# A Fourier layer tower on one core: layer 0 from raw images held as rows, and batch statistics joined in one product

## The chip, the cores and the metric

The kernel runs on one core of a Trainium2 chip. The core has TensorE (PE, the matmul array, with its weight loads shown as PEld), VectorE (DVE), ScalarE (ACT), GpSimd (POOL) and SyncE (SP, which here issues the transfers). The metric is the device time of one execution in microseconds (us); lower is better.

## The reference

The input is 32 images of 64 x 64 pixels. A tower of four Fourier layers comes first, then a small transformer and a mixture of experts, which the change doesn't touch. The tower:

```python
h = concatenate([x, gx, gy])            # pixel, row position, column position
v = h @ p_w + p_b                       # 3 -> 32 channels: the lift
for i in range(4):
    x1 = irfft2(mix(rfft2(v)[12 + 12 low rows, 12 low columns], fw1[i], fw2[i]))
    x2 = einsum("bcxy,cd->bdxy", v, w_w[i]) + w_b[i]
    v = x1 + x2
    mean, var = over batch and pixels, for each channel
    v = (v - mean) * rsqrt(var + eps) * bn_g[i] + bn_b[i]
    if i < 3: v = relu(v)
out = v @ q_w + q_b
```

## The kernel before

All data are float32. `V` holds the activations: four quadrants of 32 partitions (a quadrant holds 16 of the 64 image rows x, a partition one channel), and along the row 16 chunks (one x each) of 32 images x 64 columns. Programs are written per engine, by hand, and semaphores order them; there is no scheduler.

A layer l runs in stages.

1. **Forward transforms** (layers 1 to 3): DVE transposes pairs of images of V (L541), PE transforms y (L760), DVE transposes (L548), PE transforms x (L772), DVE writes the spectra `MZ` (L555).
2. **Mixing**: for k = 0..5, 48 products of 64 x 64 by 32 columns (L864, two passes each, so 96 in the profile), after POOL has changed a sign in the mode weights of two ky (L403); DVE transposes the result (L583).
3. **Inverse**: PE transforms x (`inverse_x`, L885), DVE spreads it into `G` (L590), and 16 **units** (q, r) follow: PE adds the inverse in y (L900) and the channel product of V (L915) in PSUM, ACT moves the sum to V with the bias (L451, two halves), DVE takes the moments (L597, four per unit: 64 groups in all).
4. **Statistics**: `bn_aggr` over the 64 groups of a partition (L615), then the mean over the four quadrants by a product with `average` (L950), a difference and a square on DVE (L618 to L620), a second product for the mean of the squares (L952), variance (L622), square root on ACT (L456), reciprocal with one Newton step, gain and bias (L625 to L632). Only then can relu (ACT L430) start the next layer. This is done after layers 0, 1 and 2. Layer 3 has another way.

Layer 0 differs. Its input v is an affine map of three features, so its spectra come from the images' spectra: PE transforms the images (L739, L744), and for each of 12 ky DVE and POOL multiply the image's spectrum by the lift's row (L528, L412), DVE adds the fixed part of the position features (L531) and transposes (L533), and mixing of k waits for 2k + 2 of them (`s_min`). For the units' channel product V holds the four features (pixel, x, y, one) in rows 0..3 of each quadrant, as 16 transfers of 4 partitions (L360, 120 KB each), in part queued between the mode weights, and a last four (L373) that wait on SP for the spectra, since chunk 15 of V is workspace until then. PE waits for `s_feat[q]` and `s_feat_last` before a unit. The stationary operand is `lift_w`, 4 rows by 32.

## Time and profile before

| | us |
|---|---|
| median of 3 runs | 824.98 (822.92 to 828.79) |
| the profiled execution, its own time | 826.26 |
| its span, first to last instruction | 824.5 |
| PE busy | 631.6 (77%) |
| DVE busy | 576.0 (70%) |
| ACT busy | 362.3 (44%) |
| POOL busy | 72.1 (9%) |

Busy shares are means over stages with different limits, so the stages of layer 0 and the ends of layers are read from the timeline. In a timeline a row is the start, the length, the engine, the line, what is written from what, and in brackets how long the engine had been idle and what ended that. `f32 x96` in a PE row counts passes, two for a product of float32. A row of the view by windows gives busy time of each engine and the granted TensorE clock, as a share of 2.4 GHz.

### The profile page before, as it was taken

What the parts mean: (1) busy time and instruction counts of PE and PEld (TensorE: products, weight loads), DVE (VectorE), ACT (ScalarE), POOL (GpSimd) and SP (SyncE); (2) the same over time, 40 slices, a digit from 0 to 9 for tenths busy, and PEclk for the clock granted to TensorE, in tenths of its full rate; (3) what the DMA queues carried; (4) which work ended last, traced back from release to release, by engine and by line L of the source; (5) the groups of instructions that cost most, each with busy time, mean ns of one, the idle gap of its engine ahead of it and who ended that gap; (6) DMA issues with size and microseconds to landing.
All of it is one profiled execution on the core that took longest, in us unless ns stands there. A gap on an engine that the chain in (4) does not pass through costs nothing. (4 is left out here: it accounts for less than half of the span.)

```text
span 824.5 us, 25191 instructions
## 1 busy us (share of the span) xinstructions
PE 631.6 (77%) x11575; PEld 444.5 (54%) x11575; DVE 576.0 (70%) x896; ACT 362.3 (44%) x517; POOL 72.1 (9%) x112
## 2 busy tenths in 40 slices
PE   3447997466789992666799937788595899999997
PEld 2335775132477771333777723332434787787854
DVE  6852887699448776996468778988731868567453
ACT  0002545870014555900045545737222677767753
POOL 3601000000300000001100000002000222212200
PEclk9986998699879995999699978999987999999999
...
DMA packets 14809, 28.94 MB, mean 35 GB/s; under 512 B 5664, under 2 KB 6304, under 8 KB 14688
## 3 DMA queue, kind: packets, MB, share of 16 engines
...
q10 hardware_dynamic: 288, 0.73, 0.3%
...
## 5 line engine op out<-in xcount | busy, mean ns | idle before, releaser
L451 ACT ACTIVATE V<-ps,wts 128x1024 f32<-128x1024 f32 x96 | 101.8, 1111 | 285.7 <-PE ps L900 285.7
L597 DVE BATCH_NORM_STATS2 stats<-V 128x6 f32<-128x512 f32 x192 | 117.9, 676 | 31.9 <-ACT V L451 31.9
L900 PE MATMUL ps<-tab,A 64*128 64x128 f32 x1536 | 106.7, 285 | 28.8 <-DMA V<-in_grid 17.1
L900 PEld LDWEIGHTS ps<-tab,A 64*128 64x128 f32 x1536 | 93.6, 192 | 52.8 <-issue 37.4
L541 DVE STREAM_TRANSPOSE A<-V 128x2048 f32<-128x2048 f32 x48 | 107.2, 2270 | 6.2 <-ACT V L430 6.2
L430 ACT ACTIVATE V<-V,small 128x2048 f32<-128x2048 f32 x48 | 96.1, 2080 | 5.0 <-DVE small L632 5.0
L772 PE MATMUL ps<-A,tab 128*128 128x384 f32 x192 | 68.3, 499 | 33.2 <-DVE A L548 33.2
L760 PE MATMUL ps<-A,tab 32*32 32x512 f32 x1536 | 61.3, 655 | 38.6 <-DVE A L541 38.6
L590 DVE STREAM_TRANSPOSE A<-ps 128x2048 f32<-128x2048 f32 (+1 forms) x27 | 55.4, 2070 | 42.9 <-PE ps L885 42.9
L772 PEld LDWEIGHTS ps<-A,tab 128*128 128x128 f32 x192 | 34.4, 189 | 76.7 <-DVE A L548 62.0
L548 DVE STREAM_TRANSPOSE A<-ps 128x1024 f32<-128x1024 f32 x48 | 56.3, 1210 | 11.2 <-PE ps L760 11.2
L403 POOL TENSOR_SCALAR A<-A,tab 128x384 f32<-128x384 f32 x32 | 21.1, 662 | 474.2 <-DMA A<-in_modes 474.2
L760 PEld LDWEIGHTS ps<-A,tab 32*32 32x32 f32 x1536 | 21.4, 107 | 67.4 <-issue 65.5
L864 PE MATMUL ps<-MZ,A 64*64 64x32 f32 x1536 | 40.0, 270 | 17.2 <-issue 6.1
L864 PEld LDWEIGHTS ps<-MZ,A 64*64 64x64 f32 x1536 | 38.8, 197 | 19.5 <-issue 13.5
L915 PE MATMUL ps<-V,wts 32*32 32x256 f32 x2048 | 47.8, 385 | 0.0
L583 DVE STREAM_TRANSPOSE MZ<-ps 128x1024 f32<-128x1024 f32 x18 | 22.0, 1238 | 25.9 <-PE ps L864 25.9
L885 PE MATMUL ps<-tab,MZ 64*128 64x128 f32 x576 | 39.9, 291 | 0.0
L885 PEld LDWEIGHTS ps<-tab,MZ 64*128 64x128 f32 x576 | 37.6, 205 | 0.4 <-DVE MZ L583 0.2
L436 ACT ACTIVATE ps<-ps,small 128x1024 f32<-128x1024 f32 x20 | 21.7, 1087 | 30.5 <-PE ps L782 30.5
L915 PEld LDWEIGHTS ps<-V,wts 32*32 32x32 f32 x2048 | 25.9, 103 | 10.4
L1286 POOL TENSOR_SCALAR hT<-h0T,wl 128x256 f32<-128x256 f32 x32 | 17.6, 564 | 153.4 <-DVE h0T L1433 153.4
...
## 6 DMA issues: line engine op xcount, KB each, us to landing
...
A<-in_turned SPq DMA_DIRECT2D x1, 512.0 KB, 3.6
...
```

The lines of the kernel that those rows point to most:

```text
L430: nc.scalar.activation(pair, pair, ACT.Relu, bias=bias, scale=scale).then_inc(s_relu, 1)
L451: nc.scalar.activation(Vm[:, 2 * h:2 * h + 2, r, 512 * q:512 * (q + 1)], bank(half_of_u(q, r) + 2 * h, 2).rearrange("p (m n) -> p m n", m= ...
L541: nc.vector.transpose(T[n % 3].rearrange("p (k n) -> p k n", k=16), Vk[:, :, P * n:P * (n + 1)]).then_inc(s_T, 1)
L548: nc.vector.transpose(Y[:, 1024 * p:1024 * (p + 1)].rearrange("p (c i k) -> p c i k", i=4, k=8), src).then_inc(s_Y, 1)
L590: nc.vector.transpose(G[quad % 4].rearrange("p (i x o) -> p i x o", i=4, o=CH)[:, :, 4 * r0:4 * r1], bank(half_of_x(quad), 4).rearrange("p ...
L597: last = nc.vector.bn_stats(stats[:, 16 * q + 4 * r + m, :], Vm[:, m, r, 512 * q:512 * (q + 1)])
L760: last = nc.tensor.matmul(bank(i)[Q * j:Q * (j + 1), :].rearrange("p (s k c) -> p s k c", s=2, k=8), fwd_y[rows, Q * yh:Q * (yh + 1)], T3[ ...
L772: last = nc.tensor.matmul(bank((4 if l == L - 1 else 4 + 2 * (u % 2)) + pair)[:, 0:MODES * CH], fwd_x[layout][ri], y[:, :, MODES * ri:MODE ...
L864: last = nc.tensor.matmul(out.rearrange("p (i b) -> p i b", b=2), W[ky][rows, kx, :], src, start=True, stop=True, tile_position=(64 * kxh, ...
L885: last = nc.tensor.matmul(ps[:, at:at + P], MZ[rows, 1024 * k + P * quad:1024 * k + P * (quad + 1)], inv_x[layout][rows, :], start=True, s ...
L900: last = nc.tensor.matmul(ps[:, at:at + P], G[(2 * q + quad) % 4][rows, x:x + P], inv_y[rows, :], start=step < 2 and quad == 0, stop=step ...
L915: nc.tensor.matmul(out, kernel[rows, :], src, start=False, stop=False, tile_position=(Q * i, Q * j))
```

## The change

**Layer 0's features.** The four features are no longer loaded into V. Chunk 15 of V takes `l_pixels`: in each quadrant 16 rows of images (one row for each x), two rows of ones and a row of y, one transfer of 1 MB over 128 partitions. The stationary operand of a unit's channel product is one of 16 slices of `lift_k` (19 rows by 32 columns), which POOL makes from the lifted weights and a table of ones and zeros that picks the unit's x. `lift_k` lies where the weights of ky 3 were, so SP holds the load of layer 1's ky 3 until the last unit of layer 0.

**Layer 0's spectra.** PE transforms the images in x with their spectra as stationary operand, so that the pairs of images come out along partitions, and adds the positions' part in the same bank by three products of 12 rows. A product of 19 rows by 32 columns by 512 (the pairs' rows and three fixed rows, against `lift_rows`) then gives the lifted spectrum in PSUM, 48 of them for the 12 ky, and DVE transposes six blocks of 1,024 from PSUM into MZ. POOL has no part in it, and mixing of k waits for min(k + 3, 6) of the blocks.

**Transfers.** The table of spectra goes ahead of the weights, `lift_rows` (256 KB) has a semaphore of its own, and the 12 loads of mode weights go without a break, then the mask and the pixels.

**Statistics** (layers 0 to 2). The first 48 groups are aggregated while the last row of units runs, and written back as one triple (count, mean, count x variance). After the last unit DVE aggregates this triple and the 16 groups left, spreads (1, mean, variance) over four column groups by quadrant, one product with `average` brings all quadrants' triples to every partition, and a second `bn_aggr` over 12 values in PSUM joins them. The square root on ACT reads that directly. Products are fused, so that five operations follow it in place of eight. The last unit's moments start after the first half of ACT's move.

The rows that the prediction speaks of, first PE at the start of layer 0, before:

```order
L736 MATMUL ps<-wts,stats 128x32
L739 MATMUL ps<-A,tab 32x512 x4
L744 MATMUL ps<-V,tab 128x192 x2
L864 MATMUL ps<-MZ,r_ky 64x32 x96
L864 MATMUL ps<-MZ,A 64x32 x192
L885 MATMUL ps<-tab,MZ 128x128 x24
```

and now:

```order
L746 MATMUL ps<-A,tab 32x512 x4
L749 MATMUL ps<-wts,stats 128x32
L752 MATMUL ps<-V 128x128 x3
L758 MATMUL ps<-tab,V 128x128 x6
L772 MATMUL ps<-V 32x512 x48
L892 MATMUL ps<-MZ,r_ky 64x32 x96
L892 MATMUL ps<-MZ,A 64x32 x192
```

57 products stand where 2 stood ahead of the mixing, and the lift went behind the images' transform. On DVE, from the last moments of layer 0 on, before:

```order
L597 BN_STATS stats<-V 128x6 x24
L615 BN_AGGR small<-stats 128x2
L618 COPY small<-ps 128x2
L619 TENSOR_TENSOR small<-small 128x1
L620 TENSOR_TENSOR small<-small 128x1
L622 TENSOR_SCALAR small<-ps,small 128x1
L625 RECIPROCAL small<-small 128x1
L626 TENSOR_TENSOR small<-small 128x1
```

(L627 to L632 follow, six more) and now:

```order
L592 BN_STATS stats<-V 128x6 x12
L598 BN_AGGR small<-stats 128x2
L599 MEMSET stats 128x1
L600 COPY stats<-small 128x1
L601 TENSOR_SCALAR stats<-small 128x1
L592 BN_STATS stats<-V 128x6 x12
L621 BN_AGGR small<-stats 128x2
L623 SCALAR_TENSOR_TENSOR small<-small,tab 128x12
L628 BN_AGGR small<-ps 128x2
L630 TENSOR_SCALAR small<-small 128x1
L631 TENSOR_SCALAR small<-small 128x1
L633 RECIPROCAL small<-small 128x1
```

(L634 to L639 follow, four more). Four operations moved ahead of the last 12 moments.

The diff, cut:

```diff
+    pixels = np.zeros((4, Q, BATCH, S), np.float32)
+    pixels[:, 0:16] = image[:, where, :].transpose(1, 2, 0, 3)
+    pixels[:, 16:18] = 1.0
+    pixels[:, 18] = np.linspace(0.0, 1.0, S, dtype=np.float32)
+    pixels = pixels.reshape(P, BATCH * S)
...
+    lift_rows = np.zeros((4, Q, PAIRS, CH), np.float32)
+    for i in range(PAIRS):
+        lift_rows[:, i, i] = p_w[0]
+    for f, row in enumerate((p_w[1], p_w[2], p_b)):
+        lift_rows[:, 16 + f] = row
+    lift_rows = lift_rows.reshape(P, PAIRS * CH)
...
+        room = V[:, BLK * 13:BLK * 15]
+        l_yt, l_spec, l_rows, l_grid, l_mask = (room[:, a:b] for a, b in ((0, 1024), (1024, 1408), (1408, 1920), (1920, 2432), (2432, 2448)))
+        l_pixels = V[:, BLK * 15:BLK * 16]
+        lift_k = r_ky[:, KW * 3:KW * 3 + 16 * CH]
...
             sp.dma_start(l_turned, turned).then_inc(s_const, 16)
             sp.dma_start(tab[:, :], table[:, 0:T_ALL]).then_inc(s_const, 16)
+            sp.dma_start(l_grid[0:12, :], grid_spectra).then_inc(s_const, 16)
             sp.dma_start(lift, weights[:, 0:P]).then_inc(s_const, 16)
             sp.dma_start(wts[:, :], weights[:, P:P + W_PARAMS + N_PARAMS]).then_inc(s_const, 16)
-            sp.dma_start(l_rows, lift_rows).then_inc(s_const, 16)
-            sp.dma_start(l_grid, grid_spectra).then_inc(s_const, 16)
+            sp.dma_start(l_rows, lift_rows).then_inc(s_rows, 16)
...
-            for ky in range(RING):
+            for ky in range(MODES):
                 load_modes(0, ky)
-            load_features(0)
-            for ky in range(RING, MODES):
-                load_modes(0, ky)
...
-            sp.wait_ge(s_min, MODES)
...
+            sp.dma_start(l_mask, grid).then_inc(s_mask, 16)
+            sp.dma_start(l_pixels, pixels).then_inc(s_feat, 16)
             for l in range(1, L):
                 for ky in range(RING):
                     sp.wait_ge(s_mix, KYP * (l - 1) + ky // 2 + 1)
+                    if l == 1 and ky == RING - 1:
+                        sp.wait_ge(s_U, 2 * UNITS)
                     load_modes(l, ky)
...
+            nc.gpsimd.memset(l_yt, 0.0).then_inc(s_pad, 1)
+            pool.wait_ge(s_const, 80)
+            for ky in range(MODES):
                 negate(0, ky)
-            pool.wait_ge(s_lspec, 1)
-            for ky in range(MODES):
...
-                if ky >= RING:
-                    negate(0, ky)
+            pool.wait_ge(s_lyt, 2)
+            pool.wait_ge(s_mask, 16)
+            pool.wait_ge(s_mix, 2)
+            nc.gpsimd.tensor_tensor(lift_k.rearrange("p (k c) -> p k c", c=CH), lift_w[:, :].unsqueeze(1).broadcast_to([P, 16, CH]),
+                                    l_mask.unsqueeze(2).broadcast_to([P, 16, CH]), ALU.mult).then_inc(s_lift_k, 1)
...
-                act.wait_ge(s_bn, 3 * l + 3)
-                nc.scalar.activation(small[:, 10:11], small[:, 9:10], ACT.Sqrt).then_inc(s_sqrt, 1)
+                act.wait_ge(s_bn, 2 * l + 2)
+                nc.scalar.activation(small[:, 10:11], small[:, 3:4], ACT.Sqrt, bias=small[:, 23:24]).then_inc(s_sqrt, 1)
...
             nc.vector.tensor_scalar(small[:, 17:18], bn_bias[L - 2], 0.0, None, ALU.max).then_inc(s_shift, 1)
-            fixed, term = (t.rearrange("p (k c) -> p k c", c=CH) for t in (l_fixed, l_term))
+            nc.vector.memset(small[:, 20:21], 1.0)
+            link(nc.vector.memset(small[:, 23:24], EPS))
+            dve.wait_ge(s_lift, 1)
+            dve.wait_ge(s_pad, 1)
+            nc.vector.transpose(l_yt.rearrange("p (k i) -> p i k", i=Q)[:, 0:PAIRS, :],
+                                bank(0).rearrange("p (i x) -> p i x", x=Q)).then_inc(s_lyt, 1)
             dve.wait_ge(s_lift, 2)
-            nc.vector.transpose(l_yt.rearrange("p (k i) -> p i k", i=PAIRS),
-                                bank(0).rearrange("p (i x) -> p i x", x=Q)).then_inc(s_lyt, 1)
             nc.vector.tensor_copy(lift_w[:, :], bank(2)[:, 0:CH]).then_inc(s_lyt, 1)
...
-            dve.wait_ge(s_lspec, 1)
-            for ky in range(MODES):
-                grid3 = l_grid3[ky % 2].rearrange("p (i c) -> p i c", c=CH)
-                if ky % 3:
-                    dve.wait_ge(s_lift0, ky - ky // 3)
-                else:
...
-                link(nc.vector.tensor_tensor(grid3, grid3, l_fixed[:, CH * ky:CH * (ky + 1)].unsqueeze(1).broadcast_to(three),
-                                             ALU.add))
-                nc.vector.transpose(MZ[:, 512 * ky:512 * (ky + 1)], l_grid3[ky % 2]).then_inc(s_min, 1)
+            for k in range(KYP):
+                dve.wait_ge(s_outer, k // 2 + 1)
+                nc.vector.transpose(MZ[:, 1024 * k:1024 * (k + 1)], bank((4 + 2 * k) % 8, 2)).then_inc(s_min, 1)
...
                 def moments(q, r):
-                    dve.wait_ge(s_V, 2 * (UNITS * l + 4 * q + r + 1))
                     for m in range(4):
+                        if m == 0 or q == OCT - 1 and r == 3 and m == 2:
+                            dve.wait_ge(s_V, 2 * (UNITS * l + 4 * q + r) + (1 + m // 2 if q == OCT - 1 and r == 3 else 2))
                         last = nc.vector.bn_stats(stats[:, 16 * q + 4 * r + m, :], Vm[:, m, r, 512 * q:512 * (q + 1)])
                     last.then_inc(s_stats, 1)
+                def moments_so_far():
+                    dve.wait_ge(s_stats, UNITS * l + UNITS - 4)
+                    link(nc.vector.bn_aggr(small[:, 2:4], groups[:, 0:6 * 48]))
+                    nc.vector.memset(so_far[:, 0:1], 48.0 * 512.0)
+                    nc.vector.tensor_copy(so_far[:, 1:2], small[:, 2:3])
+                    nc.vector.tensor_scalar(so_far[:, 2:3], small[:, 3:4], 48.0 * 512.0, None, ALU.mult).then_inc(s_sofar, 1)
...
-                nc.vector.bn_aggr(small[:, 2:4], stats[:, :, :].rearrange("p n s -> p (n s)")).then_inc(s_bn, 1)
-                dve.wait_ge(s_bn, 3 * l + 1)
-                dve.wait_ge(s_avg, 2 * l + 1)
-                link(nc.vector.tensor_copy(small[:, 5:7], bank(0)[:, 0:2]))
-                link(nc.vector.tensor_tensor(small[:, 7:8], small[:, 2:3], small[:, 5:6], ALU.subtract))
-                nc.vector.tensor_tensor(small[:, 4:5], small[:, 7:8], small[:, 7:8], ALU.mult).then_inc(s_bn, 1)
-                dve.wait_ge(s_avg, 2 * l + 2)
-                nc.vector.tensor_scalar(small[:, 9:10], bank(1)[:, 0:1], small[:, 6:7], EPS, ALU.add, ALU.add).then_inc(s_bn, 1)
-                dve.wait_ge(s_bn, 3 * l + 3)
+                dve.wait_ge(s_sofar, l + 1)
+                link(nc.vector.bn_aggr(small[:, 21:23], groups[:, 6 * 48 - 3:]))
+                nc.vector.scalar_tensor_tensor(out=small[:, 24:36].rearrange("p (q n) -> p q n", n=3),
+                                               in0=small[:, 20:23].unsqueeze(1).broadcast_to([P, 4, 3]), scalar=4.0,
+                                               in1=pick[:, 0:Q:8].unsqueeze(2).broadcast_to([P, 4, 3]),
+                                               op0=ALU.mult, op1=ALU.mult).then_inc(s_bn, 1)
+                dve.wait_ge(s_avg, l + 1)
+                nc.vector.bn_aggr(small[:, 2:4], bank(0)[:, 0:12]).then_inc(s_bn, 1)
+                dve.wait_ge(s_bn, 2 * l + 2)
+                nc.vector.tensor_scalar(small[:, 9:10], small[:, 3:4], EPS, None, ALU.add)
+                link(nc.vector.tensor_scalar(small[:, 5:6], small[:, 2:3], -1.0, None, ALU.mult))
                 dve.wait_ge(s_sqrt, l + 1)
                 link(nc.vector.reciprocal(small[:, 11:12], small[:, 10:11]))
...
-                nc.vector.tensor_tensor(small[:, 1:2], bn_bias[l], small[:, 12:13], ALU.subtract).then_inc(s_norm, 1)
+                link(nc.vector.scalar_tensor_tensor(out=small[:, 12:13], in0=small[:, 11:12], scalar=small[:, 11:12], in1=small[:, 9:10],
+                                                    op0=ALU.mult, op1=ALU.mult))
+                link(nc.vector.tensor_scalar(small[:, 13:14], small[:, 12:13], -0.5, 1.5, ALU.mult, ALU.add))
+                link(nc.vector.scalar_tensor_tensor(out=small[:, 0:1], in0=small[:, 13:14], scalar=small[:, 11:12], in1=bn_gain[l],
+                                                    op0=ALU.mult, op1=ALU.mult))
+                nc.vector.scalar_tensor_tensor(out=small[:, 1:2], in0=small[:, 0:1], scalar=small[:, 5:6], in1=bn_bias[l],
+                                               op0=ALU.mult, op1=ALU.add).then_inc(s_norm, 1)
...
-            nc.tensor.matmul(bank(2)[:, 0:CH], lift, conv_w[0], start=True, stop=True).then_inc(s_lift, 1)
+            pe.wait_ge(s_const, 80)
             for j in range(4):
                 b2, xh = j // 2, j % 2
                 last = nc.tensor.matmul(bank(0)[Q * j:Q * (j + 1), :], front_y[:, Q * b2:Q * (b2 + 1)],
                                         l_turned[:, 512 * xh:512 * (xh + 1)], start=True, stop=True)
             last.then_inc(s_lift, 1)
+            nc.tensor.matmul(bank(2)[:, 0:CH], lift, conv_w[0], start=True, stop=True).then_inc(s_lift, 1)
+            for g in range(3):
+                nc.tensor.matmul(bank(1)[:, P * g:P * (g + 1)], l_grid[0:12, 0:P], l_grid[0:12, P * (g + 1):P * (g + 2)],
+                                 start=g == 0, stop=False)
             pe.wait_ge(s_lyt, 1)
-            for ri in range(2):
-                last = nc.tensor.matmul(bank(1)[:, 0:MODES * PAIRS], fwd_x[0][ri],
-                                        l_yt[:, MODES * PAIRS * ri:MODES * PAIRS * (ri + 1)], start=ri == 0, stop=ri == 1)
+            for g in range(3):
+                for ri in range(2):
+                    at = Q * (MODES * ri + 4 * g)
+                    last = nc.tensor.matmul(bank(1)[:, P * g:P * (g + 1)], l_yt[:, at:at + P], fwd_x[0][ri],
+                                            start=False, stop=g == 2 and ri == 1)
             last.then_inc(s_lift, 1)
+            pe.wait_ge(s_lspec, 1)
+            pe.wait_ge(s_rows, 16)
+            for g in range(3):
+                if g == 1:
+                    pe.wait_ge(s_lyt, 2)
+                if g == 2:
+                    pe.wait_ge(s_min, 2)
+                for j in range(4):
+                    for k in range(4):
+                        rows = slice(Q * k, Q * k + SPEC_ROWS)
+                        last = nc.tensor.matmul(bank((4 + 4 * g) % 8 + k)[Q * j:Q * (j + 1), :],
+                                                l_spec[rows, P * g + Q * j:P * g + Q * (j + 1)], l_rows[rows, :],
+                                                start=True, stop=True, tile_position=(Q * k, Q * j))
+                last.then_inc(s_outer, 1)
...
                     if l == 0:
-                        pe.wait_ge(s_min, 2 * k + 2)
+                        pe.wait_ge(s_min, min(k + 3, KYP))
...
-                                rows = slice(Q * i, Q * i + depth)
+                                rows = slice(Q * i, Q * i + (Q if l else PIXEL_ROWS))
                                 out = bank(base + i)[Q * j:Q * (j + 1), :].rearrange("p (s h n) -> p h s n", s=2, h=2)[:, half]
-                                src = Vm[rows, j, r, 512 * q:512 * (q + 1)].rearrange("p (s h n) -> p h s n", s=2, h=2)[:, half]
-                                nc.tensor.matmul(out, kernel[rows, :], src, start=False, stop=False,
+                                src = (Vm[rows, j, r] if l else l_pixels[rows, :])[:, 512 * q:512 * (q + 1)]
+                                chunk = 4 * j + r
+                                kernel = conv_w[l][rows, :] if l else lift_k[rows, CH * chunk:CH * (chunk + 1)]
+                                nc.tensor.matmul(out, kernel, src.rearrange("p (s h n) -> p h s n", s=2, h=2)[:, half],
+                                                 start=False, stop=False,
                                                  tile_position=(Q * i, Q * j))
...
-                    if l == 0:
-                        pe.wait_ge(s_feat[q], 64)
-                        pe.wait_ge(s_feat_last, 64)
+                    if l == 0 and q == 0:
+                        pe.wait_ge(s_feat, 16)
+                        pe.wait_ge(s_lift_k, 1)
...
-                pe.wait_ge(s_bn, 3 * l + 1)
-                nc.tensor.matmul(bank(0)[:, 0:2], average, small[:, 2:4], start=True, stop=True).then_inc(s_avg, 1)
-                pe.wait_ge(s_bn, 3 * l + 2)
-                nc.tensor.matmul(bank(1)[:, 0:1], average, small[:, 4:5], start=True, stop=True).then_inc(s_avg, 1)
+                pe.wait_ge(s_bn, 2 * l + 1)
+                nc.tensor.matmul(bank(0)[:, 0:12], average, small[:, 24:36], start=True, stop=True).then_inc(s_avg, 1)
...
```

## Rows read from the trace of the kernel before

**Rows 1.** Timeline (start us, length us, engine, line, operation): DVE at the start of layer 0

```profile
15.98 0.71 DVE L533 STREAM_TRANSPOSE MZ<-A 128x512 f32<-128x512 f32 x1
...
39.75 0.71 DVE L533 STREAM_TRANSPOSE MZ<-A 128x512 f32<-128x512 f32 x1
```

**Rows 2.** Timeline, layer 0 up to its first unit

```profile
7.72 1.94 PE L739 MATMUL ps<-A,tab 128*32 128x512 f32 x8
...
7.98 0.58 POOL L403 TENSOR_SCALAR r_ky<-r_ky,tab 128x384 f32<-128x384 f32 x1 [7.54 <-DMA r_ky<-in_modes]
...
10.82 1.65 PE L744 MATMUL ps<-V,tab 128*128 128x192 f32 x4 [1.16 <-DVE lift_w L515]
...
12.50 0.32 ACT L425 COPY V<-ps 128x192 f32<-128x192 f32 x1 [10.48 <-PE ps L744]
...
22.47 2.78 PE L864 MATMUL ps<-MZ,r_ky 64*64 64x32 f32 x96 [1.58 <-DVE MZ L533]
...
41.74 5.27 PE L864 MATMUL ps<-MZ,A 64*64 64x32 f32 x192 [5.95 <-DVE MZ L583]
...
48.92 4.58 DVE L590 STREAM_TRANSPOSE A<-ps 128x2048 f32<-128x2048 f32 x3 [0.59 <-PE ps L885]
...
67.27 2.08 PE L900 MATMUL ps<-tab,A 64*128 64x128 f32 x16 [17.06 <-DMA V<-in_grid]
```

**Rows 3.** Timeline, the same products in other stretches

```profile
155.31 4.08 PE L760 MATMUL ps<-A,tab 32*32 32x512 f32 x64 [8.99 <-DVE A L541]
...
159.43 2.38 DVE L548 STREAM_TRANSPOSE A<-ps 128x1024 f32<-128x1024 f32 x2 [2.07 <-PE ps L760]
...
164.15 2.34 PE L760 MATMUL ps<-A,tab 32*32 32x512 f32 x64 [0.57 <-DVE A L541]
...
397.32 2.90 PE L864 MATMUL ps<-MZ,A 64*64 64x32 f32 x101 [0.68 <-issue]
...
581.37 1.59 PE L864 MATMUL ps<-MZ,A 64*64 64x32 f32 x96
```

**Rows 4.** Busy time by windows (start:end, length, engines, PEclk, DMA share, GB/s)

```profile
18.00:34.00 16.00, 9.35 (x327) 8.98 (x328) 11.98 (x17) 0.00 (x0) 9.41 (x10) 1.00 0.57 154
...
67.00:77.00 10.00, 9.73 (x130) 8.26 (x132) 0.73 (x1) 2.12 (x2) 2.35 (x4) 0.50 0.05 18
216.00:220.00 4.00, 2.06 (x125) 1.95 (x126) 2.02 (x2) 0.00 (x0) 1.54 (x3) 1.00 1.01 384
396.00:400.00 4.00, 3.32 (x126) 3.20 (x124) 1.31 (x2) 0.00 (x0) 1.63 (x4) 0.50 0.54 177
580.00:584.00 4.00, 3.12 (x127) 2.47 (x126) 2.91 (x9) 0.90 (x2) 0.00 (x0) 1.00 0.01 4
```

**Rows 5.** Timeline, first unit of layer 1 and last moments of layers 1 and 0

```profile
241.90 1.16 PE L900 MATMUL ps<-tab,A 64*128 64x128 f32 x16 [2.21 <-DVE A L590]
...
310.73 2.47 DVE L597 BATCH_NORM_STATS2 stats<-V 128x6 f32<-128x512 f32 x4 [0.94 <-ACT V L451]
...
140.00 2.47 DVE L597 BATCH_NORM_STATS2 stats<-V 128x6 f32<-128x512 f32 x4 [0.94 <-ACT V L451]
```

**Rows 6.** Timeline, the statistics after layer 0

```profile
137.84 2.12 ACT L451 ACTIVATE V<-ps,wts 128x1024 f32<-128x1024 f32 x2 [1.29 <-PE ps L900]
...
142.50 1.89 DVE L615 BATCH_NORM_AGGREGATE small<-stats 128x2 f32<-128x384 f32 x1
...
145.14 0.16 DVE L618 COPY small<-ps 128x2 f32<-128x2 f32 x1 [0.75 <-PE ps L950]
...
146.92 0.16 DVE L625 RECIPROCAL small<-small 128x1 f32<-128x1 f32 x1 [0.34 <-ACT small L456]
...
148.47 31.88 ACT L430 ACTIVATE V<-V,small 128x2048 f32<-128x2048 f32 x16 [1.65 <-DVE small L632]
```

**Rows 7.** Groups by line (busy us, mean ns of one): two small operations of DVE

```profile
L648 DVE BATCH_NORM_AGGREGATE small<-A 128x2 f32<-128x144 f32 x1 | 0.8, 805 | 0.0
...
L689 DVE SCALAR_TENSOR_TENSOR small<-small 128x1 f32<-128x1 f32 x1 | 0.2, 219 | 0.0
```

107 lines of the change are left out of this document (38 added, 69 removed).

## The prediction, made before the result was known

> **What bounds the kernel now.** I read the timeline of layer 0 first, then the windows for TensorE's clock, then the end of each layer 0 to 2, because the change touches nothing else. In layer 0 DVE makes the twelve lifted spectra in a row, the first transpose at 15.98 and the last at 39.75 [rows 1]; mixing follows block by block and ends at 41.74 + 5.27 = 47.01 [rows 2]. DVE's first two spreads of the inverse would let the units begin at about 48.92 + 4.58 x 3/4 = 52.4. They begin at 67.27, and the row says why: 17.06 us idle, ended by the last feature transfer [rows 2]. So two things set the start of the units, a DVE chain and, on top, the 4-partition transfers. From the first unit to the last moments layer 0 takes 140.00 - 67.27 = 72.7 us, layer 1 takes 310.73 - 241.90 = 68.8 us [rows 2, 5] for the same units. The 3.9 us between them are the clock: it is 0.50 from 67 to 77 [rows 4], after the wait, and L900's first 16 passes take 2.08 us where they take 1.16 at the full clock [rows 2, 5].
>
> After the last unit nothing overlaps. ACT ends at 137.84 + 2.12 = 139.96, relu starts at 148.47 [rows 6]: 8.5 us, three times in the kernel, all on the path.
>
> **The clock in layer 0 needs care.** The window 18 to 34 shows 1.00, but 96 mixing passes take 2.78 us there, 29 ns each [rows 2, 4]. At 397, in a window at 0.50, they take 2.90/101 = 29 ns, and at 581, in one at 1.00, 1.59/96 = 17 ns [rows 3, 4]. So I take these early passes as run at 1.2 GHz, and the 1.00 as a value that stands before the first recorded change. The Trainium skill, "TensorE: Matmul & The Clock Gate", section "What's actually happening", says that the throttled state is the default and that activity releases it; by that rule the array starts slow, and the durations agree while the printed clock does not. Were the 1.00 right, the mixing would stay at 2.78 us per block, which is a rival below.
>
> **The change, layer 0.** Its new path, step by step.
>
> - Constants. The images' transform starts at 7.72, behind the lift's product; now it is first and the last constants are issued one transfer earlier. I take 6.9, and 1.94 us at the same price [rows 2]: 8.8. The first transpose and the gap before L744 cost 10.82 - 9.66 = 1.2 us; the lift and the three products of the positions fit in that gap. 10.0.
> - Spectra in x: 12 passes of 128 columns where there were 4 of 192 in 1.65 us [rows 2], 0.41 each. By columns that is 0.27, by passes 0.41: 3.3 to 4.9 us, and I take 3.6, since mixing passes with short streams go far faster. 13.6. ACT's copy takes 0.32 for 192 columns and now has 384, 0.5: 14.1.
> - Lifted spectra: 96 passes of 32x32 tiles by 512. 64 such passes take 4.08 us slow and 2.34 at full clock [rows 3], so a third (32) is 2.04 or 1.17. Rows used (19 or 32) don't appear in a pass's length: units with 4 rows and with 32 both give the steady pace of the moments. Two thirds end at 18.2. DVE transposes 1,024 from PSUM in 2.38/2 = 1.19 [rows 3]; the first two blocks are out at 18.6, the third part is then written by 20 to 21, and mixing can begin, as it needs only three blocks. This replaces the 24 us of rows 1. The last three transposes lie beside it.
> - Mixing: six blocks without a wait for DVE. In the trace the clock rose somewhere in the 5.27 us of back-to-back mixing, and at the latest with the 4.08 us of L760 [rows 2, 3]. Early rise: 20 + 6 x 1.59 = 29.5. Late rise: 21.2 + 5.3 for two blocks, then 4 x 1.59 = 32.9. I take 31.
> - Mode weights: twelve loads of 384 KB at the 384 GB/s of the window at 216 [rows 4] take 12.3 us behind the 256 KB of rows, so the last lands near 20.5; POOL needs 0.58 for each sign change [rows 2]. Mixing at one block per 1.59 us is never ahead of them. Mask and pixels (1 MB, 2.8 us) land by 24. `lift_k` is one POOL operation of 512 columns after the twelve sign changes, done before 28. Both are hidden by the mixing; without that cover they would move the first unit one for one.
> - Units: from the end of mixing 52.4 - 47.0 = 5.4 us, so the first at 36.4, and with a warm array layer 1's 68.8 us: last moments at 105.2 instead of 140.0. **Gain 34.8 us** (33 to 36.5 by the two clock cases).
> - SP holds the load of layer 1's ky 3 until the units are done. It is used at about 180, and only loads that wait for the forward stage stand behind it. POOL's sign changes after it wait too, but nothing asks for them earlier. Zero.
>
> **The change, statistics.** In the last row of units each group of moments follows 0.94 us of idle DVE [rows 5]. The early aggregation has 288 values. Two sizes give 1.89 us for 384 and 0.805 for 144 [rows 6, 7], thus 0.156 + 4.5 ns per value: 1.45 us, and with three small operations about 2.0. It eats the first idle stretch and 1.1 us more; the second is eaten by that, so the last moments begin when the half of ACT's last move is there, near 139.2, and end at 141.6 in place of 142.5. Aggregation of 99 values: 0.60, ends 142.2. The spread product 0.2. PE and its way back take 145.14 - 144.39 = 0.75 [rows 6]: 143.2. Aggregation of 12 values 0.21: 143.4. The root on ACT lies beside two scalar operations: reciprocal at 143.8 (before: 146.92). Eight operations took 148.47 - 146.92 = 1.55; five remain, three of them with a pointer scalar at 0.219 [rows 7], 1.15 us. Relu at 144.9: **3.5 us less**, 10.6 for three layers. Bounds: 2.5 (aggregation from PSUM or of few values dearer than the line through the two sizes) and 4.2 each.
>
> **Sum.** 826.26 (the profiled execution's own time) - 34.8 - 10.6 = 780.9. The median before is 1.3 lower, which I leave inside the range. **781 us.**
>
> **Rivals.**
> 1. The array gains no speed in the mixing of layer 0, either as the printed 1.00 is true there or as the clock does not rise. For it: the window of rows 4. Against: 29 ns against 17 ns. Six blocks take 16.7: mixing ends at 37.9, units at 43.3 to 44.1, gain 27 to 28. Total 788.
> 2. A transfer takes the place of the one removed. If the twelve loads do not reach 384 GB/s but half of it, weights and pixels land near 38, mixing ends at 34.5, units start near 40. Gain 31. Total 785.
> 3. The statistics give little: the early aggregation delays the last moments, or `bn_aggr` from PSUM is dear. 1.5 us each: total 787.
> 4. Slower than before: the units' channel products, with one image block read by four column tiles and 19 rows of weights that change with every tile, leave the array at 1.2 GHz for all of layer 0's units. L900 shows the price, 2.08/1.16 = 1.79; on 68.8 us that is +54 us, total 835. It decides against the change once 45.4/54 = 84% of the stage runs slow. For it: the first unit ran slow for 10 us though PE was busy 9.73 of them [rows 4]. Against: it did speed up with 4 rows, and 32 rows in layer 1 keep the clock.
>
> **Chances.** Forecast (774 to 787) 0.76, rivals 0.10, 0.05, 0.06, 0.03. The range 773 to 794 leaves out rival 4, a fast end where everything is at its bound, and two rivals together. A measurement here can't tell less than about 1% (8 us) from no change: faster 0.97, same 0.01, slower 0.02.
>
> **What would show it.** The first L926 row (the units' first) near 36 with a DVE releaser, not a DMA; no row of DVE between the lift's copy and the six transposes from PSUM; mixing of 96 passes at about 1.6 us in most blocks; 16 units in 68.8 us; ACT's last move to relu in 5.0 us instead of 8.5. The forecast is wrong if the first unit waits for pixels or `lift_k`, if mixing waits for mode weights, or if the clock falls between outer products and units.

## The result, and the profile after

| | before | changed |
|---|---|---|
| median of 4 runs, us | 826.47 (822.92 to 828.79) | 788.89 (787.36 to 796.71) |
| ratio | | 0.957, 95% interval 0.953 to 0.961 |
| profiled execution, us (span) | 826.26 (824.5) | 787.36 (785.6) |
| first unit of layer 0 begins | 67.27 | 43.74 |
| ACT's last move of layer 0 ends | 139.96 | 112.52 |
| relu of layer 0, 1, 2 begins | 148.47, 319.20, 489.59 | 117.35, 284.14, 452.62 |

The kernel is 4.3% faster; 781 us was forecast. Of the span's 38.9 us, 27.4 lie ahead of the last move of layer 0, 3.7 between that and relu, 3.9 and 1.9 in layers 1 and 2, and 1.9 in all that follows. The stretch from move to relu is 3.7 shorter in layers 1 and 2 as well (279.31 to 284.14 and 447.79 to 452.62, 4.83 us each); layer 2 gave only 1.9 since its way from layer 1's relu to its own last move took 163.65 us, where it was 161.88.

The start of layer 0 now, from the timeline (start us, duration us, engine, line, operation, tiles, count, and in brackets the idle time ahead with what ended it). It answers to [rows 1, 2].

```profile
7.01 1.93 PE L746 MATMUL ps<-A,tab 128*32 128x512 f32 x8 [7.01 <-DMA wts<-in_weights]
11.02 2.93 PE L758 MATMUL ps<-tab,V 128*128 128x128 f32 x12
13.98 0.48 ACT L435 COPY V<-ps 128x384 f32<-128x384 f32 x1 [11.97 <-PE ps L758]
14.51 4.09 PE L772 MATMUL ps<-V 19*32 19x512 f32 x64 [0.57 <-ACT V L435]
16.71 7.01 DVE L526 STREAM_TRANSPOSE MZ<-ps 128x1024 f32<-128x1024 f32 x6 [6.57 <-PE ps L772]
19.15 2.02 PE L772 MATMUL ps<-V 19*32 19x512 f32 x32 [0.55 <-DVE MZ L526]
21.10 5.35 PE L892 MATMUL ps<-MZ,r_ky 64*64 64x32 f32 x192
26.24 8.17 PE L892 MATMUL ps<-MZ,A 64*64 64x32 f32 x288
35.02 2.79 PE L892 MATMUL ps<-MZ,A 64*64 64x32 f32 x96 [0.61 <-issue]
37.73 3.71 PE L913 MATMUL ps<-tab,MZ 64*128 64x128 f32 x48
40.15 4.58 DVE L583 STREAM_TRANSPOSE A<-ps 128x2048 f32<-128x2048 f32 x3 [1.04 <-PE ps L913]
43.74 1.16 PE L926 MATMUL ps<-tab,A 64*128 64x128 f32 x16 [2.31 <-DVE A L583]
44.84 1.49 PE L943 MATMUL ps<-V,r_ky 19*32 19x256 f32 x64
```

DVE's 24 us chain and the wait for the last feature transfer are gone: the first unit is released by DVE's spread of the inverse, and its 1.16 us for 16 passes says full clock. The mixing begins at 21.10, the late end of the forecast's 20 to 21.2. It does not end where it was forecast: 576 passes from 21.10 to 37.81, 29 ns each on average, with one pause of 0.61 us, and no group of them faster than 27.9 ns.

The end of layer 0, same view, answers to [rows 6].

```profile
104.72 1.44 DVE L598 BATCH_NORM_AGGREGATE small<-stats 128x2 f32<-128x288 f32 x1
109.14 4.88 DVE L592 BATCH_NORM_STATS2 stats<-V 128x6 f32<-128x512 f32 x8 [0.36 <-ACT V L461]
110.40 2.12 ACT L461 ACTIVATE V<-ps,wts 128x1024 f32<-128x1024 f32 x2 [1.29 <-PE ps L926]
114.05 0.60 DVE L621 BATCH_NORM_AGGREGATE small<-stats 128x2 f32<-128x99 f32 x1
114.92 0.60 PE L979 MATMUL ps<-small,tab 128*128 128x12 f32 x2 [4.11 <-DVE small L623]
115.56 0.21 DVE L628 BATCH_NORM_AGGREGATE small<-ps 128x2 f32<-128x12 f32 x1 [0.69 <-PE ps L979]
116.20 0.16 DVE L633 RECIPROCAL small<-small 128x1 f32<-128x1 f32 x1 [0.18 <-ACT small L466]
117.35 4.08 ACT L440 ACTIVATE V<-V,small 128x2048 f32<-128x2048 f32 x2 [1.25 <-DVE small L639]
```

From the end of ACT's last move (112.52) to relu: 4.83 us where it was 8.51. Each aggregation lies on the line through the two sizes of before: 1.44, 0.60 and 0.21 us for 288, 99 and 12 values, from PSUM as from SBUF.

### The profile page after: what moved, and what is told of

Same layout as the page of the kernel before. It is cut to its first block and busy times, and to the rows that moved or that the text cites. A ratio compares the mean times of both kernels' runs of the same rounds, so it can differ in the third digit from the quotient of the medians.

```text
span 785.6 us, 25353 instructions
## 1 busy us (share of the span) xinstructions
PE 637.4 (81%) x11679; PEld 445.4 (57%) x11679; DVE 558.0 (71%) x874; ACT 362.5 (46%) x517; POOL 60.5 (8%) x106
## 5 line engine op out<-in xcount | busy, mean ns | idle before, releaser
L926 PE MATMUL ps<-tab,A 64*128 64x128 f32 x1536 | 104.3, 281 | 13.6 <-ACT V L461 7.8
L926 PEld LDWEIGHTS ps<-tab,A 64*128 64x128 f32 x1536 | 91.1, 187 | 37.4 <-issue 22.2
L801 PE MATMUL ps<-A,tab 128*128 128x384 f32 x192 | 70.0, 509 | 33.0 <-DVE A L541 33.0
L416 POOL TENSOR_SCALAR A<-A,tab 128x384 f32<-128x384 f32 x32 | 18.7, 586 | 393.1 <-DMA A<-in_modes 393.1
L892 PEld LDWEIGHTS ps<-MZ,A 64*64 64x64 f32 x1536 | 39.2, 199 | 10.8 <-issue 9.9
L943 PEld LDWEIGHTS ps<-V,wts 32*32 32x32 f32 x2048 | 25.9, 103 | 10.4
## 6 DMA issues: line engine op xcount, KB each, us to landing
V<-in_pixels SPq DMA_DIRECT2D x1, 1024.0 KB, 12.6
```

What stands on the lines that cost most here:

```text
L801: last = nc.tensor.matmul(bank((4 if l == L - 1 else 4 + 2 * (u % 2)) + pair)[:, 0:MODES * CH], fwd_x[layout][ri], y[:, :, MODES * ri:MODE ...
L892: last = nc.tensor.matmul(out.rearrange("p (i b) -> p i b", b=2), W[ky][rows, kx, :], src, start=True, stop=True, tile_position=(64 * kxh, ...
L926: last = nc.tensor.matmul(ps[:, at:at + P], G[(2 * q + quad) % 4][rows, x:x + P], inv_y[rows, :], start=step < 2 and quad == 0, stop=step ...
L943: nc.tensor.matmul(out, kernel, src.rearrange("p (s h n) -> p h s n", s=2, h=2)[:, half], start=False, stop=False, tile_position=(Q * i, Q ...
```

## Experiments: the parts alone

All are compared with the kernel before on the same chip. The first four undo or keep one part.

**The statistics alone**, on the kernel before.

```diff
+ # before with: moments_so_far(), the spread by quadrant, one product with average,
+ # the second bn_aggr, the fused products; layer 0 as it was
```

> The kernel before with the statistics of the change alone. Theory (the two halves of the change are worth what their stretches show): ACT's last move to relu takes 4.8 us instead of 8.5 after layers 0, 1 and 2, the start of layer 0 is as before (first unit at about 67), so 11 us less than before, near 815. Rival (the shorter idle of TensorE after the units changes its clock in the next forward stage): more than 13 or less than 8 us.

817.62 us (815.53 to 818.77), ratio 0.989 (0.986 to 0.992). Relu of layer 0 at 146.61, which is 1.9 us earlier in this execution, where the units' first wait and their slow clock are still there (66.57 and 2.08 us for 16 passes); the units took 2.5 us longer in this execution (the granted clock fell again at 95.9 and its mean from 96 to 112 is 0.79), so the last move ends at 141.79, 1.8 later than before, and from there to relu it is 4.82 us. The part is worth 3.7 us from move to relu in each of the three layers, 11 in all as expected, and 10.8 by the medians of these runs (828.38 before). The spans of the two profiled executions differ by 9.1 only, because of those units.

**Both parts of layer 0, old statistics**, and each of the two alone.

```diff
  # lift_only:    the change without its statistics
  # rows_only:    before + l_pixels and lift_k (spectra still by POOL and DVE)
  # spectra_only: before + lifted spectra by TensorE (features still 4 rows a quadrant)
```

> The changed kernel with the old statistics, so layer 0's rows and spectra alone. Theory: first unit near 44 as in the changed kernel, relu of layer 1 at about 121, 27.5 us less than before, near 799; with the statistics' 11 us that adds up to the change's 38.9. Rival (the two halves help each other through the clock): the two alone add up to less than 35 or more than 43.

> The kernel before with the features held as rows (one load of 1 MB, lift_k by POOL) and nothing else; the spectra are lifted by DVE and POOL as before. Theory (a transfer and a DVE chain stand one behind the other): the wait of 17 us for features goes, the first unit starts when the spreads are out, 48 to 52.4, and the slow first 10 us of the units go too if the array has just worked: 15 to 23 us less than before, near 806. Rival (the transfers were only the last of several waits): first unit after 58, less than 10 us.

> The kernel before with the spectra lifted by TensorE and nothing else; features are loaded into V by 16 transfers of 4 partitions as before. Theory: mixing is over by 40 or so, but the first unit still waits for features, which land near 60 to 67, and the array has gone slow by then: 0 to 7 us less than before, near 822. Rival (the features were late only since the last four waited for the spectra): first unit near 45, 20 us or more less.

| | median us | ratio (95%) | first unit |
|---|---|---|---|
| both | 802.53 | 0.972 (0.968 to 0.975) | 45.65 |
| rows alone | 806.93 | 0.976 (0.973 to 0.979) | 48.78 |
| spectra alone | 829.07 | 1.000 (0.997 to 1.003) | 66.15 |

The first units of these three, from their timelines:

```profile
45.65 1.16 PE L909 MATMUL ps<-tab,A 64*128 64x128 f32 x16 [2.30 <-DVE A L581]
```

```profile
48.78 1.66 PE L904 MATMUL ps<-tab,A 64*128 64x128 f32 x16 [2.30 <-DVE A L595]
```

```profile
66.15 2.08 PE L914 MATMUL ps<-tab,A 64*128 64x128 f32 x16 [25.56 <-DMA V<-in_grid]
```

The bracket decides each. The rows alone came as expected (near 806, first unit from 48 to 52.4), the spectra alone at the low end of 0 to 7 us. The spectra alone finish their mixing at 37.4 and then wait 25.56 us for the features, so they gain nothing; the rows alone remove that wait, and DVE's chain shows up behind it at 48.8. Nearly all of the gain is the rows' as long as both are counted from before, and the spectra's share, 3 to 5 us, exists only once the rows are in: two limits in parallel, of which the later one hides the other. The times of both parts and of the rows alone overlap in their intervals; the 3.1 us between their first units carry this. (Constants landed 1.5 us later in the run with both parts, 8.49 instead of 7.01, which is most of why its unit begins at 45.65 and not at 43.74.)

Do the two halves add up? Both parts of layer 0 were expected at 799 us and took 802.5. By medians they gave 25.9 us and the statistics 10.8, 36.6 together, where the change has 37.6. By the spans of the profiled executions it is 22.6 and 9.1, 31.7 of 38.9, which is below the 35 that the rival named. The rows tell where this goes: 1.5 us to the late constants, 2.5 to the slow units of the run above, and 4.2 to layers 1 and 2 of this one, whose ways from relu to last move took 163.5 and 164.8 us instead of 162.2 and 161.9. None of it lies in a stretch that a half changes, so nothing here shows the halves helping each other.

**No early aggregation**: all 384 values after the last unit.

```diff
-                    if q == OCT - 1:
-                        moments_so_far()
-                link(nc.vector.bn_aggr(small[:, 21:23], groups[:, 6 * 48 - 3:]))
+                link(nc.vector.bn_aggr(small[:, 21:23], groups))
```

> The changed kernel with all 64 groups aggregated after the last unit, the early aggregation left out, the rest of the new statistics kept. Theory (by aggregation at 0.156 us + 4.5 ns per value): 1.89 in place of 0.60, +1.3 us per layer, +3.9 in all; the early one costs nothing since the last moments wait for ACT. Rival (the early aggregation delays the last moments by part of its 2.0 us): less than +0.8 per layer.

Three runs of 791.41 to 798.37 us, ratio 0.961 (0.953 to 0.969); a fourth took 3138.08 us and is left out. The times can't tell it from the change. The rows can: last move ends at 112.70, aggregation of 384 values 1.89 us, relu at 118.82, thus 6.12 us against 4.83. The early part is worth 1.3 us in layer 0, as expected.

## Experiments: why the mixing stayed at 29 ns a pass

The forecast had the mixing speed up to 17 ns. Two theories: the clock never rose for it, or something else holds it. One run above already has the rise. With the spectra alone the clock came up inside the mixing, and yet it took from 21.02 to 37.39, 16.4 us; its last block:

```profile
35.79 1.60 PE L879 MATMUL ps<-MZ,A 64*64 64x32 f32 x96 [0.59 <-issue]
```

Ahead of this block, too, TensorE had stood, 1.01 us with no wait named and 0.55 us for POOL.

**Repeat the second third of the outer products** three times, to give the array more to do ahead of the mixing.

```diff
-                for j in range(4):
+                for j in list(range(4)) * (3 if g == 1 else 1):
```

> The changed kernel with the second third of the outer products done three times over (the same values into the same bank), which adds 4.1 us of dense work ahead of the mixing, of which 0.5 lie in a wait. Theory 1 (the clock): dense products raise it before the mixing, whose passes then take 17 ns instead of 29; +3.0 and -6.7 and -0.7, first unit near 39, total 4 us less than the changed kernel. Rival (not the clock): +3.5 us.

793.37 us, ratio 0.958 (0.953 to 0.962). 160 outer passes took 9.87 us, 62 ns each, then the mixing 24.40 to 40.86 at 29 ns; the first unit at 47.36 was slow too. The 4 us less of theory 1 did not come; the time is 4.5 us above the changed kernel, nearer to the rival's 3.5 more. In this execution the clock had not come up by then, so the run says nothing on a mixing at full clock.

**Products of zeros while the constants load.** DVE's clearing of the banks leaves out banks 4 to 7 here.

```diff
+            pe.wait_ge(s_pad, 1)
+            for n in range(40):   # 32 x 32 x 512, operands zero, into banks 4 to 7
+                nc.tensor.matmul(bank(4 + i)[Q * j:Q * (j + 1), :], l_yt[rows, 0:Q], l_yt[rows, 512:1024], ...)
```

> The changed kernel with 40 products of zeros (32x32 tiles by 512 columns, into banks that the start no longer clears by DVE) on TensorE while the constants load, 1.7 to about 6.9 us. Theory 1 (layer 0's mixing takes 29 ns a pass since the array is at its lower clock and mixing alone does not raise it): the array is at full clock by the first product or soon after and stays there, mixing passes take 17 ns, the first unit starts near 34 instead of 43.7, total 9 us less than the changed kernel. Theory 2 (the sparse stretch between 9 and 14.5 us lets it fall again): no gain. Rival (mixing in layer 0 is held by fresh weights or by the transfers, not by the clock): the first products are faster, mixing keeps 29 ns.

788.16 us, ratio 0.953 (0.949 to 0.957). From its timeline (the first row is the images' transform, 1.93 us in the changed kernel), and its windows (PE, PEld, DVE, ACT, POOL busy us and count, granted clock, DMA share, GB/s):

```profile
8.06 1.07 PE L752 MATMUL ps<-A,tab 128*32 128x512 f32 x8 [1.20 <-DMA wts<-in_weights]
12.53 2.35 PE L778 MATMUL ps<-V 19*32 19x512 f32 x64 [0.57 <-ACT V L435]
16.29 2.02 PE L778 MATMUL ps<-V 19*32 19x512 f32 x32 [1.42 <-DVE MZ L526]
18.25 4.15 PE L898 MATMUL ps<-MZ,r_ky 64*64 64x32 f32 x145
```

```profile
14.50:16.00 1.50, 0.37 (x15) 0.00 (x0) 1.50 (x2) 0.00 (x0) 0.93 (x2) 1.00 1.03 406
16.00:18.00 2.00, 1.71 (x32) 0.29 (x32) 2.00 (x3) 0.00 (x0) 1.21 (x3) 0.55 1.04 404
```

The products did raise the clock: 8 passes of the images' transform take 1.07 us in place of 1.93. The 64 outer passes in 2.35 us don't show it, for the run without the early aggregation has no such products and the same 2.35. The clock fell when the third third waited 1.42 us for DVE, and the mixing began slow again. That is what theory 2 said, no gain, by a gap in another place; the rival isn't tested, as the mixing never ran at full clock.

**Close that gap too**: the second third twice.

```diff
-                for j in range(4):
+                for j in list(range(4)) * (2 if g == 1 else 1):
```

> The early products of zeros as in the run before, and the second third of layer 0's outer products issued twice (32 passes more), so that TensorE has work until the third third may start and the granted clock does not fall ahead of the mixing. Theory 1 (the mixing keeps the full clock if it begins at it without a gap; what it cannot do is raise it): the 576 mixing passes from about 18.5 us take 17 ns each, with a pause of about 1.2 us end near 30, the first unit starts near 36 instead of 42.9, time about 782 us. Theory 2 (passes of 32 columns are too thin to keep the clock even without a gap): the clock falls inside the mixing, later passes take 29 ns, first unit at 41 to 43, about 788 us. Theory 3 (at full speed the mixing uses instructions up faster than they are supplied, pauses of one to four microseconds appear inside it with no wait named, and the clock falls at the first of them): a first stretch of 17 ns passes, then a pause, then 29 ns; first unit at 39 to 41, about 786 us.

787.38 us, ratio 0.952 (0.949 to 0.954). Timeline and windows:

```profile
16.43 1.87 PE L898 MATMUL ps<-MZ,r_ky 64*64 64x32 f32 x113
21.81 2.25 PE L898 MATMUL ps<-MZ,r_ky 64*64 64x32 f32 x76 [3.50 <-issue]
23.88 5.28 PE L898 MATMUL ps<-MZ,A 64*64 64x32 f32 x175
```

```profile
18.30:21.80 3.50, 0.01 (x1) 0.00 (x0) 2.60 (x3) 0.00 (x0) 1.86 (x4) 0.77 1.03 406
22.00:30.00 8.00, 7.57 (x276) 7.30 (x273) 2.50 (x2) 0.00 (x0) 2.77 (x4) 0.50 0.34 113
```

113 passes at 17 ns, the full clock at last, and then TensorE stands for 3.50 us in the middle of a block, where the program has no wait; the row names none ("issue"). The clock falls in that pause and the rest runs at 29 ns. This is the picture of theory 3, though later than it said (first unit at 42.39, not 39 to 41). The mixing takes 19.2 us, from 16.43 to 35.67, against 16.7 in the changed kernel.

**Keep the clock up with denser passes between**: four products of 384 columns ahead of each block, in layers 0 to 2.

```diff
+                    if l < L - 1:
+                        for par in range(2):
+                            for kxh in range(2):   # overwritten by the block's own passes
+                                nc.tensor.matmul(bank(...)[64 * par:64 * (par + 1), 0:384],
+                                                 W[2 * k + par][rows, 0, :], MZ[rows, 1024 * k:1024 * k + 384], ...)
```

> The same, and in layers 0 to 2 four products of 64 rows by 384 columns ahead of each of the mixing's six blocks (8 passes of 111 ns at full clock, as layer 3 has them beside its mixing, where the clock stays up). Their results are overwritten. At full clock they cost 0.9 us a block, 5.3 us a layer; at half clock 10.7. Theory 1: the mixing holds the clock anyway, so layer 0's mixing ends near 35 us and layers 1 and 2 stay as long as they were (18.5 us from first to last mixing pass: 9.8 of passes, 5.3 of these, 3 of pauses); about 787 us. Theory 2: they are what keeps the clock, the same times, while the run without them falls inside the mixing. If they don't keep it: passes at 29 ns with them, 27 us a layer, about 815 us. Theory 3: pauses shrink, since the engine draws fewer instructions per microsecond; the same 787 us or a little less.

793.2 us, ratio 0.958 (0.952 to 0.964). Four stretches of layer 0's mixing, each from pause to pause, and what the transfer queues carried from 24 to 38 us:

```profile
21.80:25.70 3.90, 2.59 (x128) 2.32 (x127) 1.25 (x1) 0.00 (x0) 2.06 (x3) 1.00 0.64 220
25.70:29.60 3.90, 2.59 (x127) 2.25 (x128) 1.25 (x1) 0.00 (x0) 0.70 (x2) 1.00 0.07 24
29.60:33.50 3.90, 2.60 (x128) 2.25 (x127) 1.25 (x1) 0.00 (x0) 0.00 (x0) 1.00 0.02 4
33.50:37.30 3.80, 2.59 (x127) 2.15 (x128) 1.25 (x1) 0.00 (x0) 0.00 (x0) 1.00 0.02 4
```

```profile
q8 instruction: 3, 0.05, 1.3%
```

This is the decisive picture. The clock is 1.00 throughout layer 0's mixing and each stretch holds 2.59 us of work, yet it takes 3.9: after every 128 passes and as many weight loads comes a pause of 1.2 to 1.3 us, wherever in a block that falls (104 passes long here). In each stretch one transfer of 0.02 MB passes on the queue that carries instructions. I read this as the array at full speed using its program up faster than the program arrives. The Trainium skill, "Advanced Engine Details and Errata", section "ISA Cache", gives cache lines of 16 KB, 256 instructions, "Only 2 cache lines!", and 128 KB of cache on TensorE. 128 passes with 128 weight loads are 256 records, and the three packets of the row have 0.05 MB, so the trace agrees with the size of a line; how many lines TensorE has, no run here shows. In the runs with idle transfer engines 128 passes take 3.4 to 3.9 us from pause to pause. No run does the same work with fewer instructions, so the cause rests on the count, on the packets and on the pauses' staying when passes are denser or wider (below), not on an edit that takes it away.

The denser passes held the clock in layer 0 only. In layer 1 it fell at 194.5, in a pause of 2.32 us, and in layer 2 at 365.1, and from there the added passes cost twice as much: so 793.2 us and not the 787 expected.

**Is it the mode weights' transfers?** Layers 1 and 2 show such a pause in the changed kernel, 3.55 and 3.81 us; layer 1's timeline and windows:

```profile
185.72 2.40 PE L892 MATMUL ps<-MZ,r_ky 64*64 64x32 f32 x146 [1.07 <-DVE MZ L548]
191.67 1.39 PE L892 MATMUL ps<-MZ,r_ky 64*64 64x32 f32 x44 [3.55 <-issue]
192.88 9.59 PE L892 MATMUL ps<-MZ,A 64*64 64x32 f32 x335
```

```profile
186.00:188.00 2.00, 2.00 (x142) 2.00 (x135) 0.61 (x1) 0.00 (x0) 1.06 (x3) 1.00 0.98 381
188.00:192.00 4.00, 0.45 (x19) 0.34 (x17) 0.64 (x1) 0.00 (x0) 1.87 (x4) 0.69 1.02 407
```

```diff
+                if l in (1, 2):   # 64 of 768 columns; the rest of the weights is leftover data
+                    sp.dma_start(W[ky]...[:, 0:2 * CH], modes[l * MODES + ky][:, 0:2 * CH])...
```

> The changed kernel with the mode weights of layers 1 and 2 not loaded but for the first 64 of their 768 columns (each transfer a twelfth), so the mixing of these layers computes with leftover numbers. The mixing of layer 1 begins at full clock at 185.7 us, stops for 3.55 us at 188.1 with no wait named while the transfers run at 400 GB/s, and goes on at 29 ns a pass. Theory 3 (the supply of instructions stands behind the data in the same transfer engines): without the data the pause goes to under 1 us, the clock stays, 576 passes take 9.8 us and layers 1 and 2 are each about 7 to 8 us shorter, 773 us. Rival (the pause has another cause, a wait for the sign change of a weight for one): sign changes come early here too, so this rival also gains, but a pause remains in a stretch where they are done. Second rival (passes of 32 columns can't keep the clock): no pause but the clock falls all the same, 3.5 us a layer gained at most, 782 us.

784.43 us, ratio 0.949 (0.946 to 0.952). Its layer 1:

```profile
185.98 2.40 PE L895 MATMUL ps<-MZ,r_ky 64*64 64x32 f32 x146 [1.08 <-DVE MZ L551]
189.47 0.84 PE L895 MATMUL ps<-MZ,r_ky 64*64 64x32 f32 x44 [1.09 <-issue]
190.15 1.39 PE L895 MATMUL ps<-MZ,A 64*64 64x32 f32 x80
192.93 2.95 PE L895 MATMUL ps<-MZ,A 64*64 64x32 f32 x128 [1.39 <-issue]
196.63 4.94 PE L895 MATMUL ps<-MZ,A 64*64 64x32 f32 x174 [0.76 <-issue]
```

Between theories it is a half, and only in layer 1: the first pause went from 3.55 to 1.09 us, so data in the transfer engines does hold the instructions up (by one execution; the other runs built on the changed kernel have 2.32 to 3.95 us here), but a pause after each 128 passes stays (128 passes per 3.46 and 3.70 us), and the clock falls all the same at 193.8. Layer 1 gained 3.0 us from last move to last move, not the 7 to 8 that theory 3 stated; its number was wrong since I had put the whole supply down to contention. Layer 2 gained nothing: its first pause is 0.80 us where it was 3.81, but the next one, from 355.8 on, lasts 5.22 us, with 267 GB/s moving from 354 to 358; the loads of layer 3 kept their size.

**Twice the columns in each pass of layer 0**, as many passes, on the kernel with the gap closed.

```diff
+                                d = 2 if l == 0 and kx + 1 < MODES else 1
-                                out = bank(...)[64 * par:64 * (par + 1), BATCH * kx:BATCH * (kx + 1)]
+                                out = bank(...)[64 * par:64 * (par + 1), BATCH * kx:BATCH * (kx + d)]
```

> The kernel with the early and the repeated products; in layer 0 each mixing pass streams 64 columns instead of 32 (the second 32 are overwritten by the pass that follows), so the passes and their weight loads are as many as before, 576 and 576. Theory 3 (what bounds the mixing is the supply of TensorE's instructions: one transfer of 0.02 MB for every 128 passes, which takes 3.5 to 3.9 us from pause to pause whatever the clock): from the second pause on, 128 passes still take 3.5 to 3.9 us, the last mixing pass ends at 35 to 36 us as in the run with 32 columns (35.6), first unit 42 to 43, time 787 us. Rival (the array's clock and columns bound it: 64 columns take 18.5 ns at full clock by the 111 ns of 384 columns, 37 ns at half clock): after the clock has fallen the remaining 450 passes take 37 ns instead of 29, the mixing ends 3.5 us later, near 39, and the time is about 791 us. Both agree if the denser passes keep the clock up through the pause; then the pauses show it: 18.5 ns passes with a pause after each 128.

784.73 us, ratio 0.950 (0.948 to 0.953).

```profile
16.42 2.04 PE L900 MATMUL ps<-MZ,r_ky 64*64 64x64 f32 x113
21.36 1.33 PE L900 MATMUL ps<-MZ,r_ky 64*64 64x64 f32 x73 [2.90 <-issue]
25.50 3.16 PE L900 MATMUL ps<-MZ,A 64*64 64x64 f32 x127 [1.96 <-issue]
29.12 2.43 PE L900 MATMUL ps<-MZ,A 64*64 64x64 f32 x127 [0.46 <-issue]
32.55 1.44 PE L900 MATMUL ps<-MZ,A 64*64 64x64 f32 x81 [1.00 <-issue]
```

Double the columns and the mixing ends at 33.99, 1.7 us earlier than with 32. The rival's 3.5 us later did not come, and its 37 ns a pass at half clock neither: 127 passes took 3.16 us, 25 ns each, in a stretch whose granted clock is 0.62. Columns are no part of the price here; 128 passes take 4.14, 3.62 and 3.43 us from pause to pause, and the pauses fill whatever the array leaves. The 1.7 us are not the columns' gift: the clock stood at 1.00 through the first two pauses, and the first of them took 2.90 us instead of 3.50 with the same transfers beside it.

**Transfers out of the instructions' way**: the pixels after half of the mixing, the next layer's first weights after all of it.

```diff
+            sp.wait_ge(s_mix, 3)
             sp.dma_start(l_pixels, pixels).then_inc(s_feat, 16)
-                    sp.wait_ge(s_mix, KYP * (l - 1) + ky // 2 + 1)
+                    sp.wait_ge(s_mix, KYP * l)
```

> The kernel with the early and the repeated products; the pixels' transfer is issued only when half of layer 0's mixing is done (about 27 us; 1 MB alone lands by 31 us, needed at 42), and each next layer's first four transfers of mode weights only when the whole mixing of the layer before is done. So from 20.5 us on no data stands in the transfer engines ahead of TensorE's instructions. Theory 3: the first pause (3.5 us at 18.3, with the pixels' and the weights' transfers ahead of it) shrinks to 1.5 to 2.5 us since only the mode weights are left ahead of it, the mixing ends 1 to 2 us earlier and the units follow; layers 1 and 2 gain up to 0.5 us each; about 785 us. Rival (the pause has nothing to do with the transfers of data): all as before, 787.4 us.

785.25 us of 6 runs (782.23 to 787.87), ratio 0.950 (0.947 to 0.953). The first pause is 2.71 us instead of 3.50, the first unit begins at 41.73 instead of 42.39. Theory 3 wanted a first pause of 1.5 to 2.5 us, a mixing 1 to 2 us shorter and up to 0.5 us in each of layers 1 and 2. The pause is longer than that, the mixing 0.5 us shorter, and layer 1's first pause has 3.95 us in both runs. From 18.3 to 21.1 only 38 GB/s moved, against 406 GB/s from 18.3 to 21.8 with the gap closed, yet the pause went down by just 0.8 us, and the wide passes had 2.90 us without this edit. The times can't tell it from 787.38 (0.949 to 0.954) either, and 2.9 of the 3.1 us between the two profiled spans lie behind layer 2's relu. So this edit shows an effect of the transfers on layer 0 that is 0.8 us at most, and none on layers 1 and 2. This and the wide one are the fastest versions that compute the reference, some 0.5% below the changed kernel's median, whose interval (0.953 to 0.961) touches theirs; no run had them side by side.

The mixing of layer 0, collected:

| kernel | first to last pass, us | length | clock in it |
|---|---|---|---|
| changed | 21.10 to 37.81 | 16.7 | 1.2 GHz by 29 ns a pass |
| spectra alone | 21.02 to 37.39 | 16.4 | 29 ns, then 17 ns for the last third |
| outer products repeated | 24.40 to 40.86 | 16.5 | 1.2 GHz by 28 to 29 ns a pass |
| no early aggregation | 20.08 to 37.41 | 17.3 | 0.50 |
| zeros | 18.25 to 36.36 | 18.1 | 0.50 |
| gap closed | 16.43 to 35.67 | 19.2 | full for 113 passes, then 0.50 |
| transfers late | 16.31 to 35.03 | 18.7 | full for 113 passes, then 0.50 |
| wide passes | 16.42 to 33.99 | 17.6 | full, 0.50 from 26.3 to 29.7, full |
| dense passes between | 16.53 to 37.55 | 21.0 (5.3 are theirs) | 1.00 |

At neither clock did it take less than 16.4 us, or 15.7 if the 5.3 us of the dense passes are taken off.

## Why the prediction was right, and where not

The time is inside the range of 773 to 794, but not in the 774 to 787 that held 0.76 of the chance: it is the case of rival 1, which had 0.10. That rival gave 37.9, 43.3 to 44.1 and 788 us for the end of the mixing, the first unit and the time; measured are 37.81, 43.74 and 788.9. Two of the signs that the forecast named, a first unit near 36 and blocks of 1.6 us, did not come. By step:

- **Up to the mixing: right.** Mixing from 21.10 against 20 to 21.2. The images' transform ran from 7.01 to 8.94 (6.9 to 8.8 forecast); the gap behind it was 2.1 us, not 1.2, filled by the lift (0.64) and the positions' products (1.65); spectra in x took 2.93 us (3.6, and less than the 3.3 by columns); and the outer products ran slow as assumed, 64 ns. Two errors, 0.9 us more and 0.7 less, nearly cancel.
- **Hidden work: right.** `lift_k` at 26.65, pixels landed 12.6 us after their issue at 10.37, the last sign change at 19.58; no engine waited for them. Rivals 2 and 4 did not come: DMA ran at 402 to 423 GB/s from 10 to 20 us, and 64 passes of 19 rows take 1.49 us, as with 4.
- **"I take 31": wrong, by 6.8 us.** The step read "early rise ... late rise" and had no case in which a full clock is worth nothing. Two things failed. The clock did not rise inside the mixing, as rival 1 said. And had it risen, the mixing would have taken about the same time, as the other runs show: 16.4 us where it rose for the last third, 17.6 with the wide passes, and 21.0 with the dense ones between, of which 5.3 are theirs by the estimate of 111 ns each. At 17 ns a pass 576 passes are 9.8 us. I put the rest down to the supply of instructions. Rival 1 was right in its number, but it put the 29 ns down to the clock alone. This stood in the profile of before: I took 17 ns from a row of 96 passes in layer 3, where the clock is 1.00, and did not read on. These are that layer's next stretches there, from pause to pause, in its windows:

```profile
584.70:588.40 3.70, 2.59 (x127) 2.32 (x127) 3.01 (x5) 1.75 (x4) 0.00 (x0) 1.00 0.02 4
588.40:592.10 3.70, 2.59 (x127) 2.32 (x127) 1.98 (x3) 0.90 (x2) 0.00 (x0) 1.00 0.02 4
```

  3.70 us for 127 recorded passes, eight of them of 384 columns, is 29 ns a pass at full clock, too. The window at 216 of [rows 4], which the prediction used for its 384 GB/s, ends in such a pause, at clock 1.00; its row in the timeline of before:

```profile
220.71 1.92 PE L864 MATMUL ps<-MZ,r_ky 64*64 64x32 f32 x66 [1.83 <-issue]
```

  A mean of one group inside a stretch is no rate of the stretch.
- **Units: right.** 5.9 us from the last mixing pass to the first unit (5.4), then 68.8 to the end of the last move, as taken from layer 1. So layer 0 gave 27.4, of 34.8 forecast, and the 7.4 missing are the mixing's 6.8 and this 0.5.
- **Statistics: right, a little low.** Rival 3 did not come: 3.7 us from move to relu in each of the three layers, against 3.5. By their relus layers 1 and 2 gave 5.9 us together (7.0 forecast), as layer 2 lost 1.8 us on its way to its last move, and the rest of the kernel gave 1.9. No step of mine holds these two; by chance they cancel. The runs of the parts show the same stretches of layers 1 and 2 anywhere from 161.9 to 164.8 us.
- **Both halves of layer 0 as one sum: not tested by it.** The runs show that one half alone is worth nothing and the other some 20 us (21.5 by medians, 18.8 by spans).
